# The place of 32 counting products and the order of SyncE's transfers before the first batch

## The reference

```python
x = x + tanh(g_xattn[0]) * L0_xattn(layernorm(x), ctx, w_qkv, w_proj, b_proj)   # 16 heads, 256 + 120 keys
x = x + tanh(g_ffn[0])   * L0_ffn(layernorm(x), weight, bias)                   # ternary weights, one global scale
x = x + tanh(g_xattn[1]) * L1_xattn(layernorm(x), ctx, patch_lens, W_in, ...)   # below
x = x + tanh(g_ffn[1])   * L1_ffn(layernorm(x), rhs)                            # int8 by row and column
```

```python
bidx = cumsum(patch_lens, axis=1) - 1
boundary_mask = zeros((bsz, seqlen)).at[arange(bsz)[:, None], bidx].set(1)
plug = clip(cumsum(boundary_mask, axis=1) - 1, 0, plen - 1)
depool_out = depool[arange(bsz)[:, None], plug]
```

## Time and profile before

| | us |
|---|---|
| median of 3 runs | 1075.43 (1074.79 to 1076.40) |
| the profiled execution | 1076.64 |
| its span | 1074.8 |
| TensorE busy | 1037.7 (97%) |
| VectorE busy | 874.6 (81%) |
| ScalarE busy | 793.1 (74%) |
| GpSimd busy | 694.4 (65%) |
| mean granted TensorE clock | 0.99 |

### The profile page before, as it was taken

The page is one execution under the profiler, slowest core; times in us unless marked ns, Lnnn a source line. Parts: engine busy times, 40 slices in busy tenths (PEclk is TensorE's granted clock), DMA queues, the critical chain, the costliest instruction groups (busy, mean ns, idle before and its releaser), DMA issues. The chain is left out here.

```text
span 1074.8 us, 26415 instructions
## 1 busy us (share of the span) xinstructions
PE 1037.7 (97%) x8627; PEld 706.5 (66%) x8627; DVE 874.6 (81%) x2219; ACT 793.1 (74%) x1731; POOL 694.4 (65%) x1347
## 2 busy tenths in 40 slices
PE   5999999999999999999999999999999998999994
PEld 3466666666666666666666666666666555888883
DVE  7777888788888888887788888888887876999997
ACT  3377777777777777777777777777777665999983
POOL 5566666666666666666666666666666414688876
PEclk9899999999999999999999999999999999999997
DMA  6855555566555555556555555655555311233332
GB/s 143 137 105 108 111 108 108 107 108 107 109 111 114 111 109 109 107 108 107 108 109 111 110 111 110 110 109 112 98 103 101 59 45 34 66 113 98 115 107 87
DMA packets 140908, 111.31 MB, mean 104 GB/s; under 512 B 15650, under 2 KB 136932, under 8 KB 140772
## 3 DMA queue, kind: packets, MB, share of 16 engines
q1 hardware_dynamic: 140185, 109.16, 50.0%
q10 hardware_dynamic: 587, 0.47, 0.2%
HBM read 30.33 MB, written 16.32 MB: 43 GB/s over the span
## 5 line engine op out<-in xcount | busy, mean ns | idle before, releaser
L980 DVE TENSOR_REDUCE neg<-ms_ps 128x1 f32<-128x376 f32 x1024 | 525.6, 543 | 156.5 <-PE ms_ps L733 150.9
L1069 ACT ACTIVATE probs<-st_ps 128x512 f32<-128x512 f32 x768 | 442.4, 603 | 23.5 <-PE st_ps L723 22.8
L733 PE MATMUL ms_ps<-qk 96*128 96x376 bf16 x1024 | 332.8, 325 | 3.1 <-DVE neg L980 2.5
L723 PE MATMUL st_ps<-qk 99*128 99x256 bf16 x1536 | 294.4, 273 | 0.5 <-DMA qk<-negT 0.5
L723 PEld LDWEIGHTS st_ps<-qk 99*128 99x128 bf16 x1536 | 133.0, 98 | 125.7 <-issue 40.8
L748 PE MATMUL pv_ps<-probs,v 128*32 128x256 f32 (+1 forms) x3072 | 194.5, 383 | 0.0
L771 PE MATMUL misc<-xnT,wqkvT 128*128 128x256 f32 x512 | 154.7, 387 | 1.7 <-DVE wqkvT L862 0.9
L733 PEld LDWEIGHTS ms_ps<-qk 96*128 96x128 bf16 x1024 | 98.4, 96 | 69.7 <-DVE neg L980 48.7
L748 PEld LDWEIGHTS pv_ps<-probs,v 128*32 128x32 f32 (+1 forms) x3072 | 96.2, 110 | 55.8 <-ACT probs L1069 12.8
L565 POOL TENSOR_SCALAR parts<-qk 128x632 bf16<-128x632 f32 x63 | 45.5, 722 | 127.9 <-ACT qk L1142 127.9
L1076 ACT COPY negT<-aux 24x256 bf16<-24x256 bf16 x64 | 22.9, 358 | 102.2 <-PE aux L789 102.2
(11 more groups left out here) (235 smaller groups left out, 1759.4 us busy)
## 6 DMA issues: line engine op xcount, KB each, us to landing
qk<-parts SPq DMA_DIRECT2D x254, 94.0 KB, 3.6
qk<-parts SPq DMA_DIRECT2D x128, 158.0 KB, 3.7
qk<-parts SPq DMA_DIRECT2D x256, 64.0 KB, 3.5
out_dram<-xn SPq DMA_DIRECT2D x32, 256.0 KB, 2.3
xs<-in_x SPq DMA_DIRECT2D x31, 256.0 KB, 2.9
cx<-in_ctx SPq DMA_DIRECT2D x32, 240.0 KB, 4.0
recurrence_input<-u_in SPq DMA_DIRECT2D x32, 120.0 KB, 2.8
plug<-plugs SPq DMA_DIRECT2D x32, 120.0 KB, 3.4
```

Of the source, the lines that this page charges most:

```text
L723: mm = pe.matmul(st_ps[u % SR][:, j * S:(j + 1) * S], k6[0:KM, r, h, k * P:(k + 1) * P], q6[0:KM, r, h, :], start=True, stop=True)
L733: pe.matmul(ms_ps[t][:, 0:KEYS], q6[0:KR, r, h % HU, t * P:(t + 1) * P], k6[0:KR, r, h % HU, 0:KEYS], start=True, stop=True).then_inc(s_ms, 1)
L980: dve.tensor_reduce(neg[:, m, t, h % HU:h % HU + 1], ms_ps[t][:, 0:KEYS], AX.X, ALU.max, negate=True).then_inc(s_red, 1)
L1069: act.activation(probs[:, u % PR, :], st_ps[u % SR][:, :], ACT.Exp).then_inc(s_exp, 1)
```

## The change

The counting products move from step 5 to step 15 of body -1, which puts them among the maxima of batch 0, and ACT's copy of the counts with them from step 6 to step 16. SP's list in body -1 becomes: part 0 of the first half's stack of batch 1 (five DMAs), the context of batch 2, the counts' write, the rows of the first half's maxima of batch 0 (which ACT no longer issues), the other five DMAs of that stack, the kept input, x of batch 4, the counts' read, and the second half's stack.

```diff
-        AT_COUNTS = 5
+        AT_COUNTS = 15
...
-                if b == -1:
+                def maxima_first():
+
+                    load_cx()
                     sp.wait_ge(s_counts, 2)
                     sp.dma_start(count_dram.rearrange("b (h l) -> h b l", l=HEX), counts_sb[:, :, :]).then_inc(d_counts, 16)
-                    stack(1, par, 0)
+                    rows_0()
+
+                if b == -1:
+                    stack(1, par, 0, maxima_first)
+                    keep_input()
+                    load_x()
                     sp.wait_ge(d_counts, 16)
                     sp.dma_start(steps[:, 0, :], count_dram).then_inc(d_counts, 16)
-                    load_cx()
-                    keep_input()
-                    load_x()
                     stack(1, par, 1)
                     return
...
                     if u == AT["neg0"] and live(b + 1):
                         neg_rows(b + 1, i + (par + 1) // 2, opp, 0)
-                        if b == -1:
-                            wait_taken(act, b, "neg0")
-                            act.dma_start(q6[KR:KM, 2 * opp, :, :], negT[:, 0, :]).then_inc(d_neg[2 * opp], 16)
```

## The result

The changed kernel is slower by about what was forecast: 1077.61 us median (1075.31 to 1079.64, 16 runs) against 1074.99 (1074.08 to 1077.89, 16 runs), ratio 1.0019 with the 95% interval 1.0012 to 1.0027, that is +2.0 us (1.3 to 2.9). The two medians lie 2.6 apart and the two means 2.2; the text goes by the ratio. The forecast of 1076.9 stood on a median of three runs, 1075.43, so the difference is the fairer comparison. The profiled execution of the changed kernel took 1077.15, with a span of 1075.3.

The account below looks back on a forecast made before the run. TensorE, full over the long middle, was taken as the bound, so shifts at the start arrive whole. Terms −4.1 + 0.65 + 0 + 3.5 + 1.5 = +1.5 us on 1075.43 gave 1076.9, range 1073.8 to 1079.4.

Parts of the forecast that it names:

- What bounds the kernel: TensorE busy 787.72 of 790 us in the long middle, so a microsecond won or lost before it arrives whole.
- Products out of step 5: TensorE no longer waits for the digits; q's copy, k products and first scores come earlier: −4.1 us, ends 3.2 and 4.8.
- Products inside the maxima: The 32 products behind the tenth maximum's scores make VectorE stand: +0.65 us, ends 0.3 and 0.96.
- The rows' DMA on SyncE at 0: Issuing batch 0's maxima rows from SyncE instead of ScalarE costs 0, between −0.2 and +0.3 us.
- The read: Counts' read, late on SyncE after T (end of batch 0's negated maxima copy), stalls VectorE, then TensorE: +3.5 us, ends 3.1, 5.2.
- The clock: After TensorE's new stand of about 4.0 us in batch 0 the clock falls to half: +1.5 us, ends 0 and 2.7.
- No clock cost: Rival: no clock cost after the new stand; sum 0.0, 1075.4 us; chance 0.17.
- The clock falling twice: Rival: clock falls under the k products and again after the stand in batch 0: +3.6, 1079.0 us; chance 0.20.
- The gain kept: Rival: counts back in time or VectorE's stand under 1 us: −3.5, 1071.9 us; chance 0.08.
- batch 0's second stack: Landed by 37.8 us, wanted by the 17th maximum at 38.8 at the earliest, so covered.

Follow-up runs that it names:

- the early read: Changed kernel with the wait for the counts' write and the counts' read right behind the maxima's rows, ahead of the stack's last five DMAs: 0.9972 to the kernel before.
- the fillers: Changed kernel with 17 filler products ahead of the fourth scores of batch 0, where TensorE stood: ratio 1.0005 to the kernel before.
- the later index: Changed kernel with VectorE's three small index instructions in steps 6 to 8 of batch 0 instead of 0 to 2: ratio 0.9972 to the kernel before.
- both cures: Changed kernel with the counts' read right behind the rows and the index instructions in steps 6 to 8 of batch 0: ratio 0.9975 to the kernel before.
- the rows on ScalarE: Changed kernel with the maxima's rows of batch 0 issued by ScalarE again, the rest of SyncE's new order kept: ratio 1.0004 to the kernel before.
- the order alone: Changed kernel with the counting products back in step 5, leaving SyncE's new order: ratio 1.0059 to the kernel before.
- the place alone: Kernel before with only the counting products moved to step 15, SyncE's old order and the rows on ScalarE kept: ratio 1.0000.
- step 11: Changed kernel with the read behind the rows and the counting products in step 11, behind four fillers instead of eight: ratio 0.9973 to the kernel before.

## Why the prediction was right

The forecast was +1.5 us, with 0 to +3 as its own range, by an exchange of one wait for another and a fallen clock; measured are +2.0 (1.3 to 2.9). The mechanism was the one forecast, and part of the agreement is luck: in the traces the first term was 0.8 us better than forecast, and the gap in the maxima, the stand and the clock were 0.2 to 0.3 worse each.

*What bounds the kernel.* The middle passes a shift on nearly whole: 1.20 us at the first value products, 1.45 at 867 us. Right here, but only to some tenths in a single execution, and less so behind the early read, where 3.63 at the first value products had become 2.0 at 867.

*Products out of step 5.* Forecast -4.1 between the ends -3.2 and -4.8; the trace shows -4.94, just past the end at which the clock holds. The mechanism was as told (q's copy behind the square, k at full clock); I took the middle where the clock in fact held in this trace, 0.8 off, and the first scores stood at 30.05 (29.06 + 0.99), just ahead of the 30.2 to 31.8 that were to show it. In the profiled executions with the products in step 15 or 11 TensorE stood 1.7 to 2.4 us there, and in none did the clock fall.

*Products inside the maxima.* Forecast +0.65, in the trace +0.85. VectorE had less cover than one maximum less 0.2 us.

*The rows' DMA on SyncE at 0.* Right, but on a condition that the prediction didn't name: no stack DMAs beside the rows. In the changed kernel the DMA engines were empty when they went out; with the early read they still ran at full share at 41.2 and were all but idle a microsecond later. Both times the rows were there within 2.7 us. In the kernel before they went out on ScalarE's queue at 45.26 and were there within 2.7 too, with no DMA issued by SyncE between 43.4 and 46.5. Issued on ScalarE beside the stack's DMAs, the same rows landed after 5 to 5.7 us and cost as much as had been won.

*The read.* Forecast: out at T + 4.95, landed at T + 8.0, stand 3.5. Trace: T + 5.23 (the kept input's issue took 0.59, not 0.40), L913 at T + 8.34, stand 3.76. The read landed 3.1 us after its issue, as the x load just ahead of it did; alone in an empty queue the same read took 1.7. Three other runs with the read behind the x load show the same, 3.5 us for the read and 3.5 for the load, 3.7 and 3.8, 4.0 and 4.2: the read lands on the heels of the load. The prediction's two ways of pricing it were the ring order of the Trainium skill's "DMA: Bandwidth & Descriptors" (Queues, rings and completion order), with 3.5 to 3.7, and the read's own row of before, 3.1 (7.65 - 4.49 is 3.16); the first was nearer, and the traces agree with it.

*The clock.* Forecast +1.5; 1.77 in the trace, 1.5 (0.2 to 2.8) by the fillers. The half clock lasted 6.8 us again, as in the kernel before, 1.7 of them in the stand.

*The rivals.* No clock cost: ruled out by the granted clock and by the fillers. The clock falling twice: its second half happened, its first didn't. The gain kept: it is what the read behind the rows and the later index reach, 0.9972, so the term that decided was the right one. The chances of slower, same and faster by over 0.2% lay 0.31, 0.60, 0.09; the result lies at that line.

What the sum did not hold is the stack DMAs' part: batch 0's second stack was told to be covered by one us. It was covered in the changed kernel's trace, but in three others (the early read, the fillers in the stand and both cures), which are the same kernel up to there, its scores waited 0.24 to 0.27 us. These three are executions in which the launch started late (last section).

## What to carry to other kernels

In a queue written out by hand, a wait moved forward moves everything behind it back: list what stands behind it with the engine that needs each, and ask when that engine wants it. A transfer of a few KB that someone waits for should go out ahead of bulk, and when the DMA engines are running empty; in these runs which engine issued it mattered less than what was in flight. Where TensorE stands so long that the clock may fall (here it fell with stands of 1.99 to 5.00 us, and held through some of 1.7 to 2.4), price the clock as well as the stand, and if the stand can't be taken away, fill it.

## What the runs showed of the hardware that was not expected

- The time to land of a small transfer hangs on what is in flight more than on its size. The counts' read, 32 KB: 1.6 to 1.7 us alone (three runs), 2.7 behind the last stack DMAs, 3.1 to 4.0 behind the x load (four runs), 4.2 with the old order and the products in step 15, 5.0 in the run with the rows on ScalarE. The rows, 12 KB: no more than 2.7 us from either engine's queue where the DMA engines ran empty, 5.0 and 5.7 from ScalarE's queue with SyncE's stack DMAs in flight.
- The clock fell after stands of TensorE of 1.99 and 2.13 us at the start of batch 0, 0.4 to 0.5 us behind their end, but not after 1.7 to 2.4 us before the k products, nor in a stand of 2.64 us near the end until some 1.1 us after it. The length of the stand alone doesn't say whether it falls. In the stands of 2.92 to 5.00 us it fell before they ended (the kernel before, the changed kernel, the rows on ScalarE, and twice with the order alone).
- The half clock lasted 3.4 us after the two short stands and 6.8 us in each of the five long ones, counted from its fall. So what the clock costs need not grow evenly with the stand.
- The counting products, 16 columns each, took 0.96 us for 32 at either clock.
- The start of the launch scatters by up to 1.9 us between executions of kernels that are alike there, and the clock goes with it. The copy of the context keys stood at 24.6 to 25.0 in six of the twelve profiled executions (the kernel before, the early read, the fillers in the stand, the place alone, step 11, both cures) and at 23.1 to 24.0 in the other six. The first eight products with wqkvT took 3.4 to 3.8 us in the former and 1.97 in the latter; at half clock eight such products took 3.30. The packed traces hold no granted clock before 14.9 to 15.8 us in the former and 9.3 to 10.4 in the latter, and the table prints 1.00 where there is none. So the 1.00 that it shows for the start of the kernel before is not a reading, and the slow start is one in which the full clock came later; why it came later is left open.
